# Full-size TensorE products that nothing reads, in the ramp of two self-attentions and in the tail of the first

## The chip, the cores and the metric

One core of a Trainium2 chip runs the whole decoder. The metric is the device time of one execution in microseconds (us), as the median of several runs. Everything below is about that one core and its engines: TensorE (PE, with its weight loads as PEld), VectorE (DVE), ScalarE (ACT), GpSimd (POOL) and SyncE (SP), which issues the DMAs. TensorE's clock has two levels, 2.4 GHz (1.00 in the profile's rows) and 1.2 GHz (0.50); which of them it was granted stands in each row of a table of stretches.

## The reference, cut to what matters

Two decoder layers over x of 4 x 1024 x 256. The stages are L0 self-attention, L0 cross-attention, L0 experts, L1 self-attention, L1 latent attention, L1 expert choice. The two self-attentions are what the change touches. Layer 0 is causal with 16 heads of 16; layer 1 is not causal and has 32 heads of 8, in couples whose results are subtracted:

```python
scores = jnp.einsum('bhqd,bhkd->bhqk', q, k) * scale        # L0: causal, masked above the diagonal
attn = jax.nn.softmax(scores, axis=-1)
out = jnp.einsum('bhqk,bhkd->bhqd', attn, v)
# L1: the same without a mask for (q1, k1) and (q2, k2); a = attn1 - lam * attn2
```

The softmax needs the largest score of every query before the exponentials, so the kernel computes the scores twice: once for the maxima, once, shifted by them, for the exponentials.

## The kernel before, in words

`attend` (line 338) does both self-attentions. The heads are taken in groups of four: 16 groups in L0 (4 batches x 4), 32 in L1. It is one program for each engine, all written out turn by turn by `run`: turn g does the maxima of group g ("new"), the exponentials and sums of group g-1 ("last") and the rest of those of group g-2 ("old"):

```python
for g in range(groups + 2):
    turn(At(g, None, 3), g < groups, 1 <= g <= groups, g >= 2)
```

A turn has NS steps, 12 in L0 and 16 in L1. In each step the PE program (`turn`, in `@block.tensor`) goes through s = 0 to 3, and for each s it issues one score of the group in hand (`score`, L727: keys as weights, 512 queries as columns, 64 rows in L0 and 32 in L1), one product for the maxima (`most`, L777: 62 or 30 rows, up to 512 columns), and after s = 1 and s = 3 half a step of the sums (`products`, `product`, L748: exponentials times V, four heads side by side on 32 columns of the array each). The two `most` of one pair fill one psM buffer, of which there are two; VectorE reduces it (L683; in L0 the pairs on the diagonal go through L677, which adds the mask), and the next pair but one waits for that on `m_read`. A turn has 2 NS pairs. The scores go to a ring of four psS banks, which ScalarE empties with the exponentials (L600) into `parts[0]` to `parts[2]`. In L0, POOL cuts the diagonal blocks of them (L563), and `product` waits for that.

The exponentials of a group begin LATE = 5 steps into the next turn, since its maxima first have to reach Q: after step 0 of that turn PE transposes them (`turn_maxima`, L786), ScalarE and POOL split them in two, SP copies them by eight DMAs into rows of Q (L508), and PE waits for those on `mx` at step 5. So there are three kinds of turn:

- **The ramp**, turn 0: maxima of group 0 alone. In turn 1, steps 0 to 4 are maxima alone as well (those of group 1); from step 5 on, scores, maxima and sums are mixed.
- **The turns between**: everything at once.
- **The tail**, turn `groups`: no maxima. Steps 0 to 4 are the last steps of the last group but one, steps 5 to 11 (in L0) the first steps of the last group. A short turn follows for its remaining steps.

Twice in a turn PE transposes a finished sum with four full 128 x 128 products (`turn_back`, L766). `parts[3]` is used in `project`, the stage before, for the projected queries and keys, and by nothing in `attend`. The psS banks are all free in turn 0.

Of the kernel before, what the change touches and what calls it, by code (L numbers as in the profile page):

```python
# [17 lines left out]
P = 128  # L18
# [4 lines left out]
HALF = 512  # L23
# [314 lines left out]
def attend(nc, a, keep, sems, tag, dh, groups, causal):  # L338
# [23 lines left out]
    pairs = []  # L362
# [5 lines left out]
    for s, (t, h) in order:  # L368
        keys = (t + 1) * P if causal else S
        n = min(HALF, keys - h * HALF)  # L370
        pairs.append((s, t, h, n, causal and h * HALF + n == keys))
    NS, NP2 = len(steps), len(pairs)
# [9 lines left out]
    with ExitStack() as ctx:  # L382
        m = Mem(nc, ctx)
        psM = [m.ps(f"{tag}_attn_psM{k}", 2 * HALF) for k in range(2)]
        psS = [m.ps(f"{tag}_attn_psS{k}", HALF) for k in range(4)]
# [36 lines left out]
        m_read = sems.sem(f"{tag}_attn_m_read")  # L422
# [6 lines left out]
        def run(turn):  # L429

            for g in range(groups + 2):
                turn(At(g, None, 3), g < groups, 1 <= g <= groups, g >= 2)

        def cuts(g, n):

            return g.times(4 * sum(diagonal), 4 * sum(diagonal[:n]))

        def in_turn(new, last):

            return range(NS if new or last else LATE + BACK + 4)  # L440

        taken, left, s_at = [], [], {}
        for g in range(1, groups + 2):
            new, last, old = g < groups, g <= groups, g >= 2
# [33 lines left out]
        def s_item(*key):  # L478

            return s_at[key], bank_of[key]  # L480

        def m_item(g, p):

            return g * NP2 + p, (g * NP2 + p) % 2

        with nc.Block() as block:
            @block.sync
            def _(sp):
                sp.dma_start(mask[:], a["causal"]).then_inc(maskin, 16)
                if shared == 2:  # L490
                    sp.dma_start(lam4[:], a[f"{tag}_lambda"].rearrange("(o k) d -> o k d", o=1).broadcast_to([P, 4, dh])).then_inc(lamin, 16)

                def turn(t, new, last, old):
                    if new and t.base >= 1:
                        if t.base == 3:
                            for k in range(4):
                                sp.wait_ge(parts_out[k], 256)
                        if t.base >= 3:
                            sp.wait_ge(s_done, s_at[t.base - 3, NS - 1, 3] + 1)
                        load_group(sp, keep, dh, t.base)  # L500
                    if last:

                        g = t + -1
                        sp.wait_ge(m_cut, g.times(2, 2))
                        for s in range(4):
                            c, r = head(s)
                            for j in range(2):
                                sp.dma_start(Q[g.slot][r + TOP + j:r + TOP + j + 1, c, :].bitcast(F32),  # L508
                                             mparts[g.slot][s * TB:(s + 1) * TB, j, :].bitcast(F32)).then_inc(mx[g.slot], 16)

                run(turn)
                for k in range(3):
                    n = len(range(k, groups, 3))
                    sp.wait_ge(mx[k], 128 * n)
# [202 lines left out]
            @block.tensor  # L717
            def _(pe):
                pe.sem_inc(o_done, RING)

                def score(g, n, s):
                    q, kt, c0 = steps[n]
                    c, r = head(s)
                    i, bank = s_item(g.base, n, s)

                    pe.wait_ge(e_done, order[g.base, n, s] + 1)
                    pe.matmul(psS[bank][:, c0:], K[g.slot][r:r + RH, c, kt * P:(kt + 1) * P],  # L727
                              Q[g.slot][r:r + RH, c, q * HALF + c0:(q + 1) * HALF], start=True, stop=True).then_inc(s_done, 1)

                def product(at, n, half):  # L730
                    g = At(at, None, 3)
                    q, kt, c0 = steps[n]
                    lo, hi = max(c0, half * HALF // HALVES), (half + 1) * HALF // HALVES
                    if lo >= hi:
                        return
                    if lo == c0:
                        if n == 0 or steps[n - 1][0] != q:

                            pe.wait_ge(e_done, order["O", at, q] + 1)
                        if n == 0:  # L740
                            pe.wait_ge(v_in, g.times(1, 1))

                        if diagonal[n]:
                            pe.wait_ge(e_cut, cuts(g, n + 1))
                        else:
                            pe.wait_ge(e_done, freed[at, n, 3])
                    for s in range(4):
                        last = pe.matmul(psS[bank_of["O", at, q]][32 * s:32 * s + 32, lo:hi], V[g.slot][:, kt, s // shared, :],  # L748
                                         E[(4 * n + s) % (4 * RING)][:, lo:hi], start=(kt == 0 and half == 0), stop=(n == ends[q]),
                                         skip_group_check=True)  # L750
                    if half == HALVES - 1:
                        last.then_inc(o_done, 1)

                def products(t, n, last, old, half):
                    j = n - LATE - BACK
                    if j >= 0 and last:
                        product(t.base - 1, j, half)
                    if j < 0 and old:
                        product(t.base - 2, NS + j, half)

                def turn_back(g, q):
                    i, bank = s_item("B", g, q)
                    pe.wait_ge(e_done, freed["O", g, q])
                    pe.wait_ge(e_done, order["B", g, q] + 1)
                    for j in range(4):
                        last = pe.transpose(psS[bank][:, j * P:(j + 1) * P], oT[q][:, j * P:(j + 1) * P], ident[:])  # L766
                    last.then_inc(s_done, 1)

                def most(t, p, j):
                    s, qt, h, n, _ = pairs[p]  # L770
                    i, bank = m_item(t.base, p)
                    if j == 1:

                        if i >= 2:
                            pe.wait_ge(m_read, i - 1)
                    c, r = head(s + j)
                    last = pe.matmul(psM[bank][:, j * HALF:j * HALF + n], Q[t.slot][r:r + TOP, c, qt * P:(qt + 1) * P],  # L777
                                     K[t.slot][r:r + TOP, c, h * HALF:h * HALF + n], start=True, stop=True)
                    if j == 0:
                        last.then_inc(m_done, 1)  # L780

                def turn_maxima(g):
                    i, bank = s_item("T", g)
                    pe.wait_ge(m_neg, g + 2)
                    pe.wait_ge(e_done, order["T", g] + 1)
                    pe.transpose(psS[bank][0:4 * TB, 0:P], negm[g % 3][:], ident[:]).then_inc(s_done, 1)  # L786

                def turn(t, new, last, old):
                    if new:
                        pe.wait_ge(ld[t.slot], t.over(LD, LD))  # L790
                    for n in in_turn(new, last):
                        k = n - LATE
                        g, step = (t + -1, k) if k >= 0 else (t + -2, NS + k)
                        live = last if k >= 0 else old
                        if last and k == 0:
                            pe.wait_ge(mx[g.slot], g.over(128, 128))
                        for s in range(4):
                            if live:
                                score(g, step, s)
                            if new:  # L800
                                most(t, 2 * n + s // 2, 1 - s % 2)
                            if (s + 1) * HALVES % 4 == 0:
                                products(t, n, last, old, (s + 1) * HALVES // 4 - 1)
                        if last and n == 0:
                            turn_maxima(t.base - 1)
                        if old and n == BACK1:
                            turn_back(t.base - 2, 1)
                        if last and n == BACK0:
                            turn_back(t.base - 1, 0)

                run(turn)
LAMBDA_INIT = 0.8 - 0.6 * math.exp(-0.3 * 12)
BLK = 4
# [2288 lines left out]
```

## Time and profile before

| | |
|---|---|
| median of 3 runs | 3541.02 us (3540.13 to 3545.2) |
| the profiled execution's own time | 3554.61 us |
| its span, from the first to the last instruction | 3552.9 us |
| mean granted TensorE clock | 0.92 |
| PE busy | 3169.2 us (89%) |
| DVE busy | 2786.6 us (78%) |
| ACT busy | 2104.8 us (59%) |
| L0 `attend`, first maximum to last sum | about 137 to 635 us of the span |
| L1 `attend` | about 1287 to 2557 us |

Busy time of PE counts any matmul in flight, at whichever clock. A matmul's duration is its latency: several overlap, so what one costs in a stream is the distance from one start to the next.

### The profile page before, as it was taken

To read this page: it belongs to the slowest core of one execution; us is meant where nothing else is said; L and a number is where in the kernel's file an instruction comes from. 1 tells how busy PE (TensorE), PEld (TensorE's weight loads), DVE (VectorE), ACT (ScalarE), POOL (GpSimd) and SP (SyncE) were. 2 spreads that over 40 slices of the span, in tenths; PEclk is the share of its full clock that TensorE was granted. 3 is DMA by queue.
4 is the path that set the end of the run, shared out by engine and by line. 5 is a ranking of instruction groups with operands and counts; after the bars stand their busy time and mean duration, and the time that the engine had idled before them with its cause. 6 is when DMAs were issued, how large, how long until landed. Compare 5 with 4: busy or idle time off the path is not lost. (4 is left out here: it accounts for less than half of the span.)

```text
span 3552.9 us, 63589 instructions
## 1 busy us (share of the span) xinstructions
PE 3169.2 (89%) x23976; PEld 1628.0 (46%) x23976; DVE 2786.6 (78%) x4742; ACT 2104.8 (59%) x4195; POOL 870.6 (25%) x1299
## 2 busy tenths in 40 slices
PE   7599999678499879999999999999856699999699
PEld 4244444444288533333333333343345455454556
DVE  7688885447577898999999999999366677776456
ACT  3178887245333217999999999999815333334130
POOL 4234433134333430000000000000112334445100
PEclk9689999879699977999999999999978899999789
DMA  5422220000000330100100001000002410100001
GB/s 170 127 54 62 66 58 20 27 0 1 25 1 1 118 113 20 29 20 21 29 20 24 25 20 28 22 20 20 4 9 81 169 50 28 48 26 1 17 0 48
DMA packets 69587, 144.08 MB, mean 41 GB/s; under 512 B 20864, under 2 KB 33984, under 8 KB 69152
## 3 DMA queue, kind: packets, MB, share of 16 engines
q1 hardware_dynamic: 64928, 135.82, 12.9%
q8 instruction: 189, 3.10, 0.4%
q10 hardware_dynamic: 4352, 4.20, 0.3%
q14 instruction: 118, 0.97, 0.1%
HBM read 83.19 MB, written 54.53 MB: 39 GB/s over the span
## 5 line engine op out<-in xcount | busy, mean ns | idle before, releaser
L600 ACT ACTIVATE L_parts<-L_attn_psS 128x512 f32<-128x512 f32 (+3 forms) x2816 | 1410.3, 574 | 151.1 <-PE L_attn_psS L727 109.4
L683 DVE TENSOR_REDUCE L_attn_tops<-L_attn_psM 128x2 f32<-128x1024 f32 x1152 | 1326.4, 1218 | 62.4 <-PE L_attn_psM L777 59.1
L777 PE MATMUL L_attn_psM<-L_K,L_Q 30*128 30x512 f32 (+4 forms) x2816 | 869.0, 492 | 67.6 <-PEq L199 31.7
L727 PE MATMUL L_attn_psS<-L_Q,L_K 32*128 32x512 f32 (+4 forms) x2816 | 880.8, 477 | 1.6 <-ACT L_parts L600 0.9
L748 PE MATMUL L_attn_psS<-L_parts,L_attn_V 128*32 128x256 f32 (+1 forms) x10752 | 860.0, 392 | 5.5 <-ACT L_parts L600 0.6
L727 PEld LDWEIGHTS L_attn_psS<-L_Q,L_K 32*128 32x128 f32 (+1 forms) x2816 | 410.0, 186 | 558.8 <-ACT L_parts L600 274.4
L777 PEld LDWEIGHTS L_attn_psM<-L_K,L_Q 30*128 30x128 f32 (+1 forms) x2816 | 391.1, 190 | 114.3 <-DVE L_attn_tops L683 58.2
L748 PEld LDWEIGHTS L_attn_psS<-L_parts,L_attn_V 128*32 128x32 f32 x10752 | 215.0, 108 | 357.0 <-issue 189.0
L677 DVE CUSTOM_DVE_ANT_0 L_attn_psM<-L_attn_psM,L_attn_wide 128x384 f32<-128x384 f32 (+3 forms) x512 | 236.7, 523 | 20.2 <-PE L_attn_psM L777 19.7
L2357 ACT ACTIVATE x_E<-x_psS 128x512 f32<-128x512 f32 x256 | 139.0, 596 | 173.6 <-PE x_psS L2480 154.2
L2403 DVE TENSOR_REDUCE x_tops<-x_psM 128x2 f32<-128x1024 f32 x128 | 153.1, 1206 | 87.2 <-PE x_psM L2509 87.1
L2319 POOL TENSOR_TENSOR x_acc<-x_acc,x_E 128x512 f32<-128x512 f32 x128 | 172.1, 1344 | 171.5 <-ACT x_E L2357 169.2
L1557 PE MATMUL m_psE<-m_wp,m_xp 128*128 128x512 f32 x768 | 182.1, 394 | 2.8 <-DVE m_z L1691 2.8
L563 POOL TENSOR_SCALAR_AFFINE_SELECT L_parts<-L_parts 128x128 f32<-128x128 f32 x512 | 146.3, 294 | 129.9 <-ACT L_parts L600 123.2
L554 POOL TENSOR_TENSOR L_attn_mparts<-L_attn_mT,L_attn_mparts 32x128 fp32r<-32x128 f32 x48 | 21.6, 450 | 623.9 <-ACT L_attn_mT L609 623.9
L542 POOL TENSOR_TENSOR L_attn_recs<-L_attn_rec,L_attn_sign 128x16 f32<-128x16 f32 x64 | 14.3, 223 | 634.1 <-DVE L_attn_rec L694 634.1
L1557 PEld LDWEIGHTS m_psE<-m_wp,m_xp 128*128 128x128 f32 x768 | 142.6, 189 | 34.6 <-DVE m_z L1691 5.8
L2476 PE MATMUL x_psS<-x_Q,x_K 64*128 64x512 f32 x864 | 148.0, 431 | 11.6 <-ACT x_E L2357 11.4
L2529 PE MATMUL x_psO<-x_E,L1x_VL 128*64 128x512 f32 x512 | 139.9, 625 | 0.0
L2509 PE MATMUL x_psM<-x_K,x_Q 64*128 64x512 f32 x768 | 117.9, 405 | 24.5 <-DMA x_K<-L1x_kTc 21.4
L324 PE MATMUL L_proj_psQ<-L_AO,L_proj_wqk 128*128 128x512 f32 x256 | 124.1, 611 | 16.9 <-DMA L_AO<-in_L_sin 12.6
L2476 PEld LDWEIGHTS x_psS<-x_Q,x_K 64*128 64x128 f32 x864 | 73.7, 186 | 139.8 <-ACT x_E L2357 91.7
(370 smaller groups left out, 4083.6 us busy)
## 6 DMA issues: line engine op xcount, KB each, us to landing
parts_q<-L_parts SPq DMA_DIRECT2D x64, 256.0 KB
parts_k<-L_parts SPq DMA_DIRECT2D x64, 256.0 KB
L_Q<-parts_q SPq DMA_DIRECT2D x192, 64.0 KB
L_K<-parts_k SPq DMA_DIRECT2D x192, 64.0 KB
L_Q<-parts_q SPq DMA_DIRECT2D x64, 128.0 KB
L_K<-parts_k SPq DMA_DIRECT2D x64, 128.0 KB
queries<-x1p_qo SPq DMA_DIRECT2D x16, 512.0 KB, 3.8
keys<-x1p_ko SPq DMA_DIRECT2D x16, 512.0 KB, 4.2
```

What stands on the lines that cost most here:

```text
L563: pool.affine_select(block, block, [[1, P]], ALU.is_ge, 0.0, base=0, channel_multiplier=-1).then_inc(e_cut, 1)
L600: act.activation(E[(4 * n + s) % (4 * RING)][:, c0:], psS[bank][:, c0:], ACT.Exp, scale=scale).then_inc(e_done, 1)
L677: last = dve.tensor_tensor_reduce(part, part, wide[:, HALF - n:], 1.0, LOWEST, ALU.add, ALU.max, tops[:, row, h:h + 1])
L683: dve.tensor_reduce(dst, src, AX, ALU.max).then_inc(m_read, 1)
L727: pe.matmul(psS[bank][:, c0:], K[g.slot][r:r + RH, c, kt * P:(kt + 1) * P], Q[g.slot][r:r + RH, c, q * HALF + c0:(q + 1) * HALF], start=Tr ...
L748: last = pe.matmul(psS[bank_of["O", at, q]][32 * s:32 * s + 32, lo:hi], V[g.slot][:, kt, s // shared, :], E[(4 * n + s) % (4 * RING)][:, l ...
L777: last = pe.matmul(psM[bank][:, j * HALF:j * HALF + n], Q[t.slot][r:r + TOP, c, qt * P:(qt + 1) * P], K[t.slot][r:r + TOP, c, h * HALF:h * ...
L1557: last = pe.matmul(psE[e][:], xp[u.slot][:, i, c, k * P:(k + 1) * P], wp[:, j, c, e * HALF:(e + 1) * HALF], start=(n + c == 0), stop=(n == ...
L2319: pool.tensor_tensor(to[:], to[:], e[:], ALU.add).then_inc(sums[1], 1)
L2403: dve.tensor_reduce(dst[:, :, t, h], src, AX, ALU.max).then_inc(m_read, 1)
L2476: pe.matmul(banks[h][:], K[k][rows, x, kt * P:(kt + 1) * P], Q[k][rows, y, cols], start=(j == 0), stop=False, skip_group_check=True)
L2529: last = pe.matmul(psO[LD * h:LD * h + LD, :], v, tile(s, h)[:], start=(kt == 0), stop=(kt == TB), skip_group_check=True)
```

## The change

`busy(bank)` is one matmul with a full 128 x 128 block of `parts[3]` as weights and 512 columns of it, all of the type of Q and K, into a bank that nothing reads. It is issued in two places of PE's `turn`:

- in turn 0 of both layers, after each pair of maxima, once for every full 256 columns of the pair (0, 1 or 2 times), into psS[3]: in L0 32 in all (of the 12 pairs of each half, six have 512 columns, two 384, two 256, two 128), in L1 64, two for each of the 32 pairs;
- in turn 16 of L0, after s = 1 and after s = 3 of each of the 12 steps, once, into half of psM[0]: 24. The first of them has a wait of its own ahead of it, until VectorE has read the last maxima.

```diff
+                def busy(bank):
+
+                    idle = keep["parts"][3]
+                    pe.matmul(bank, idle[:, 0, 0:P], idle[:, 0, HALF:], start=True, stop=True, skip_group_check=True)
+
                 def turn_maxima(g):
...
                             if new:
                                 most(t, 2 * n + s // 2, 1 - s % 2)
+                            if new and not last and s % 2 == 1:
+                                for _ in range(pairs[2 * n + s // 2][3] // 256):
+                                    busy(psS[3][:])
+                            if causal and last and not new and s % 2 == 1:
+                                if n == 0 and s == 1:
+                                    pe.wait_ge(m_read, groups * NP2)
+                                busy(psM[0][:, 0:HALF])
                             if (s + 1) * HALVES % 4 == 0:
                                 products(t, n, last, old, (s + 1) * HALVES // 4 - 1)
```

Nothing is removed or moved.

## Rows read from the trace of the kernel before

**Rows 1.** The page: PE busy, and its clock in 40 slices.
```profile
PE   7599999678499879999999999999856699999699
PEclk9689999879699977999999999999978899999789
```

**Rows 2.** Stretches of L0 and L1 `attend`: length, busy us (instructions) of engines, clock.
```profile
core 0: us, PE busy (x) PEld busy (x) DVE busy (x) ACT busy (x) POOL busy (x), PEclk, DMA share, GB/s
137.00:167.00 30.00, 14.93 (x48) 6.86 (x48) 24.06 (x70) 0.00 (x0) 4.18 (x8) 0.50 0.29 80
167.00:178.00 11.00, 6.41 (x22) 3.12 (x22) 10.14 (x30) 0.43 (x2) 0.45 (x1) 0.50 0.10 26
...
1286.00:1324.00 38.00, 24.86 (x66) 9.19 (x66) 36.20 (x38) 1.49 (x2) 2.41 (x8) 0.50 0.15 43
1324.00:1334.00 10.00, 7.18 (x19) 2.39 (x18) 9.93 (x10) 0.42 (x2) 0.79 (x2) 0.50 0.05 13
1341.00:1369.00 28.00, 28.00 (x200) 7.97 (x196) 19.78 (x17) 18.09 (x34) 0.00 (x0) 0.50 0.01 1
...
1374.00:1400.00 26.00, 25.92 (x277) 10.23 (x269) 25.41 (x24) 24.68 (x50) 3.40 (x8) 1.00 0.13 33
```

**Rows 3.** Stretches by scores alone (L727): length, PE and PEld busy, clock.
```profile
178.00:201.35 23.35, 12.25 (x28) 6.50 (x28) 0.50 0.24 58
241.00:257.35 16.35, 9.68 (x28) 4.73 (x28) 1.00 0.35 98
574.70:591.15 16.45, 9.68 (x28) 4.77 (x28) 1.00 0.01 1
601.50:622.40 20.90, 10.54 (x28) 4.38 (x28) 0.59 0.00 1
563.40:574.65 11.25, 6.23 (x20) 3.07 (x20) 1.00 0.02 5
591.20:601.40 10.20, 5.14 (x20) 2.55 (x20) 1.00 0.02 6
1334.70:1373.30 38.60, 18.75 (x44) 6.78 (x43) 0.50 0.07 17
2479.50:2505.80 26.30, 13.39 (x44) 6.13 (x44) 1.00 0.01 1
```

**Rows 4.** PE in order of time, L1 ramp: start, length, what [idle before].
```profile
1291.39 0.80 PE L777 MATMUL L_attn_psM<-L_K,L_Q 30*128 30x512 f32 x2 [0.34 <-DVE L_attn_tops L683]
1292.52 0.80 PE L777 MATMUL L_attn_psM<-L_K,L_Q 30*128 30x512 f32 x2 [0.34 <-DVE L_attn_tops L683]
```

**Rows 5.** Who DVE waited for in 143 to 166 us (L0 ramp): us, times, longest.
```profile
DVE L_attn_tops L683 <- PE L_attn_psM L777: 0.8, 2, 0.4
DVE L_attn_psM L677 <- PE L_attn_psM L777: 0.8, 2, 0.4
```

**Rows 6.** PE in order of time, L1 turn 1 to 2, around the clock's rise.
```profile
1371.37 1.08 PE L748 MATMUL L_attn_psS<-L_parts,L_attn_V 128*32 128x256 f32 x8
1372.38 1.04 PE L766 MATMUL L_attn_psS<-ident,L_attn_oT 128*128 128x128 f32 x4
1373.35 0.49 PE L727 MATMUL L_attn_psS<-L_Q,L_K 32*128 32x512 f32 x1
```

**Rows 7.** PE in order of time, L0 experts: full-size products.
```profile
972.59 4.70 PE L1557 MATMUL m_psE<-m_wp,m_xp 128*128 128x512 f32 x17
...
1039.82 2.44 PE L1557 MATMUL m_psE<-m_wp,m_xp 128*128 128x512 f32 x10
```

**Rows 8.** Two stretches of L0 cross-attention, columns as in rows 2.
```profile
834.00:844.00 10.00, 7.24 (x34) 4.07 (x27) 7.23 (x10) 7.86 (x17) 5.61 (x4) 1.00 0.01 2
844.00:850.00 6.00, 6.00 (x36) 2.77 (x34) 5.42 (x13) 2.77 (x6) 3.50 (x2) 0.72 0.00 1
```

**Rows 9.** Stretches of L0's tail, columns as in rows 2.
```profile
592.00:601.00 9.00, 9.00 (x95) 3.88 (x91) 0.22 (x1) 7.97 (x22) 4.73 (x15) 1.00 0.02 6
601.00:605.00 4.00, 3.25 (x24) 1.19 (x16) 0.00 (x0) 3.08 (x8) 2.06 (x8) 1.00 0.01 3
605.00:619.00 14.00, 13.74 (x83) 5.22 (x84) 0.25 (x1) 8.93 (x22) 3.92 (x13) 0.51 0.00 1
619.00:622.00 3.00, 3.00 (x22) 0.94 (x21) 0.00 (x0) 2.17 (x4) 0.00 (x0) 0.50 0.00 0
622.00:632.00 10.00, 10.00 (x104) 4.43 (x106) 0.25 (x1) 8.48 (x21) 4.49 (x15) 0.99 0.01 2
```

**Rows 10.** PE in order of time, L0 tail, end of step 4 and start of step 5.
```profile
600.79 0.64 PE L748 MATMUL L_attn_psS<-L_parts,L_attn_V 128*32 128x256 f32 x8
601.60 0.73 PE L727 MATMUL L_attn_psS<-L_Q,L_K 64*128 64x512 f32 x3 [0.16 <-DMA L_Q<-L_attn_mparts]
```

## The prediction

> **What bounds the kernel now.** The page first: PE is busy in most slices (of 88.8 us each), and its clock is below 9 tenths in some, among them the 2nd and 3rd and the 15th and 16th [rows 1]. Those hold the starts of the two `attend` stages. The table of stretches then shows what goes on there.
>
> The L1 ramp (1286 to 1324 us) ran at 0.50 throughout, but VectorE was busy 36.20 of 38.00 us [rows 2]: it sets the pace, and the slow clock costs nothing. In order of time, the two maxima of a pair start together, take 0.80 us, and PE then sits idle for 0.34 us until VectorE has freed a buffer; a pair comes every 1.13 us (1291.39 to 1292.52) [rows 4]. Steps 0 to 4 of turn 1 look the same: VectorE 9.93 of 10.00 us, PE 7.18. Only from step 5 on does the clock matter: from 1341 to 1369 us PE was busy all 28.00 us, VectorE 19.78, ACT 18.09, still at 0.50; after 1374, at 1.00, VectorE and ACT are both near their full share [rows 2].
>
> What that costs can be read by the same piece of work at both clocks. Scores of steps 0 to 10 of group 0 of L1 (44 of them) took 38.60 us, those of group 30 took 26.30: 12.3 us. Steps 0 to 6 of group 0 of L0 took 23.35 us, of group 2 16.35: 7.0 us. In L0's tail steps 0 to 6 of the last group took 20.90 us, of the group before (with maxima beside them) 16.45: 4.45 us [rows 3]. So 23.8 us are to be had, all three in places where scores run, none in the ramps themselves.
>
> What PE did before the clock moved: in L1 it stayed at 0.50 through 28 us of gapless scores, maxima and sums, and rose right after four full-size transposes had joined them (1372.38; at 1373.35 a score takes 0.49 us) [rows 2, 6]. In the experts it rose a moment into a run of full-size products (17 in 4.70 us from 972.59) [rows 7]. So full-size work does raise it. It fell where PE was still at work but lightly: in cross-attention after a stretch with 7.24 of 10.00 us busy [rows 8], in L0's tail after 601 to 605 us with 3.25 of 4.00 [rows 9]. It isn't idleness alone that lets it fall.
>
> **The change, part by part.** One added product costs, at 1.00, the distance between such products in a stream: ten in 2.44 us, less the last one's latency of about 0.39, over nine, is 0.23 us [rows 7]; at 0.50 twice that, 0.46.
>
> *L1 ramp, 64 products.* At 0.50 a pair then takes PE 512 columns at 1.2 GHz, 0.43 us (the two maxima run side by side), and 2 x 0.46: 1.35 us against VectorE's 1.13, so 0.22 us more for each pair while the clock is low. Full-size work is then two thirds of PE's time, more than in the mix that raised the clock at 1372, so I expect it to rise within some five pairs: +1.1 us. From there PE needs 0.21 + 0.46 = 0.67 us of 1.13: nothing. Ends: 0, and 32 x 0.22 = +7.0 if it never rises. Taken: +1.
>
> *L0 ramp, 32 products.* At 0.50 all of PE's work is at most 24 x 0.43 + 32 x 0.46 = 25.0 us beside 24.06 us of VectorE's in a stretch of 30 [rows 2]; the pairs with 128 columns get none, so PE catches up. VectorE waited for PE 1.6 us in 143 to 166 [rows 5], part of which goes if the clock is high. Ends: -1.6 and +3. Taken: 0.
>
> *Turn 1 of both layers.* The added products stop with turn 0. Then come five steps of maxima alone, 11 us in L0 (167 to 178) and 10 to 11 in L1 (1324 to 1334.7), in which PE does what it did before the change: x22 and x19 instructions of 62 or 30 rows [rows 2]. At 1.00 they are half as long, so PE is at work less than the 7.24 of 10.00 us after which the clock fell in cross-attention [rows 8]. I take it that the clock is back at 0.50 before the first score at 178.0 and 1334.8, and both losses (7.0 and 12.3) stay. Taken: 0. The other end is -19.3.
>
> *L0 tail, 24 products.* The clock fell at about 605, after PE had waited for the maxima's DMAs and with small diagonal steps to do [rows 9, 10]. Two full-size products in each step are 0.46 us more work in about 2 us, and the lightest stretch is no longer light: I expect it to stay at 1.00, worth up to 4.45 us. Against it stands their own time. In steps 0 to 4, ten products, at most 10 x 0.23 = 2.3 us; ACT is busy 7.97 of 9.00 us there [rows 9], so part of it hides. The `turn_maxima` of step 0 is queued behind two of them, so the DMAs that PE waits for at 601.60 (0.16 us idle, PE had hardly arrived earlier [rows 10]) land up to 0.46 us later. Taken: +0.9. In steps 5 to 11, fourteen products, at most 3.2 us; but the 16.45 us of the group before had 28 maxima and VectorE's pace in it [rows 3], which are gone. Taken: 0 against that 16.45. The added wait on `m_read` is met: all of PE's later work is queued behind it, but VectorE has done with the maxima as turn 16 begins (one instruction of 0.22 us in 592 to 601 [rows 9]), and `turn_maxima` of the same step waits for later work of VectorE anyway. The stage after starts with the end of this chain, so a gain here is a gain of the whole. Sum of the tail: -4.45 + 0.9 = -3.5. Ends: -4.45, and -4.45 + 2.3 + 3.2 = +1.1.
>
> **Sum.** +1 + 0 + 0 - 3.5 = -2.5 us. The profiled execution took 3554.61 us (span 3552.9), 13.6 above the median; against it this gives 3552.1. The difference carries over to the median of 3541.02: 3538.5 us. A measurement of this kernel can tell about 0.2%, 7.1 us, from no change, so this is "same".
>
> **The rivals.** *A: the clock is carried through the maxima of turn 1.* Then the scores of both layers begin at 1.00, -19.3 us more: 3519. This holds if the clock falls only where PE is idle, since in 1324 to 1334 it never is for long. Against it: both falls in rows 8 and 9 came with PE at work for 72 and 81% of the time [rows 8, 9]. The Trainium skill ("TensorE: Matmul & The Clock Gate", section "Why this matters for your kernels") states just such a rule: throughput drops are avoided by leaving no long idle gaps between bursts of matmuls. By that rule this case comes out; the falls in rows 8 and 9 speak against it, and so does the 28 us of unbroken work at 0.50 against its companion, that staying busy raises the clock [rows 2]. Chance 0.12.
>
> *B: the products don't move the clock.* They are of another kind than transposes, and may count for less. Then PE paces the L1 ramp at 1.35 us a pair (+7.0), the L0 ramp loses up to 3 (say +1.5), and the tail falls to 0.50 as before, where PE is the bound (13.74 of 14.00 us busy [rows 9]) and fourteen products at 0.46 are open: +6.4, with +0.9 before. Sum +15.8: 3557. It decides from the point where less than half of that holds, since +7.1 is already slower. For it: PE has no slack at 0.50. Against: rows 6 and 7. Chance 0.1.
>
> *C: the tail gives back what it gains.* The clock stays, but in the small diagonal steps PE, not ACT, is the bound (9.00 of 9.00 us busy in 592 to 601, [rows 9]), so most of the 24 products are open: +1.1 there, +1 in L1: 3543; half of it, 3541. Chance 0.2.
>
> **How the numbers follow.** My forecast has 0.58. Its own range is 3534 to 3543: the tail's -4.45 with -1.6 of the L0 ramp below, the spread of runs (5 us here) around it. C lies inside it. The range of 3530 to 3547 holds both, 0.78, and the nearer part of B and A's edge. Faster by over 0.2% (below 3533.9): A, and 0.08 of the forecast's lower edge, 0.2. Slower (above 3548.1): B, 0.1. The rest, 0.7.
>
> **What would show it.** In the profile after: the clock rises in each ramp (1.00 for most of 1295 to 1324), VectorE's pair stays at 1.13 us; the clock is 0.50 again by 1334 and the 44 scores of L1's group 0 still take about 38 us, the 28 of L0's about 23; in L0's tail there is no fall at 605 and the last group's 28 scores take about 16.5 us. I am wrong if group 0's scores take 26 us (A), if the ramp of L1 is longer by 5 us or more (B), or if the tail's 28 scores take over 19 us at a high clock (C).

## The result

The changed kernel took 3582.16 us (median of 4 executions, 3579.7 to 3585.45) against 3543.11 us for the kernel before (4 executions, 3540.13 to 3550.42): a ratio of 1.0101, 95% interval 1.0084 to 1.0118. By that ratio it is 36 us slower (the two medians are 39 us apart), where 2.5 us faster was forecast. The profiled execution took 3579.7 us, its span 3578.0.

The stretches of the changed kernel, columns as in rows 2; the first two answer to the L1 ramp and to steps 0 to 4 of turn 1 there, the last two to rows 9:

```profile
1294.00:1353.00 59.00, 59.00 (x128) 24.83 (x126) 39.20 (x37) 1.49 (x2) 1.63 (x7) 0.50 0.08 20
1353.50:1363.50 10.00, 6.81 (x21) 2.53 (x21) 9.50 (x11) 0.42 (x2) 0.78 (x2) 0.50 0.08 19
...
596.00:608.00 12.00, 12.00 (x100) 4.72 (x92) 0.00 (x0) 8.14 (x22) 5.08 (x16) 1.00 0.01 3
609.00:627.00 18.00, 18.00 (x128) 7.93 (x127) 0.25 (x1) 13.67 (x31) 5.20 (x17) 1.00 0.00 1
```

Two things are to be seen. The L1 ramp is now 60 us long instead of 37, PE is busy in all of it and VectorE in two thirds: PE has become the pace. And the clock is still 0.50, for all 59 us. Who VectorE waited for in that stretch (us in total, times, longest):

```profile
DVE L_attn_tops L683 <- PE L_attn_psM L777: 20.3, 32, 0.9
```

PE in order of time in the ramp, the changed kernel (L785 is the added product):

```profile
1312.14 0.79 PE L777 MATMUL L_attn_psM<-L_K,L_Q 30*128 30x512 f32 x2
...
1312.86 1.22 PE L785 MATMUL L_attn_psS<-L_parts 128*128 128x512 f32 x2
...
1314.01 0.28 PEld L777 LDWEIGHTS L_attn_psM<-L_K,L_Q 30*128 30x128 f32 x2 [0.65 <-issue]
1314.01 0.79 PE L777 MATMUL L_attn_psM<-L_K,L_Q 30*128 30x512 f32 x2
```

A pair comes every 1.87 us (1312.14 to 1314.01; 1.13 in rows 4). The two maxima have 0.43 us of columns, yet the first full-size product starts 0.72 us after them (1312.14 to 1312.86). The next maxima start 1.15 us after that (1312.86 to 1314.01), for 2 x 0.43 us of columns. So 3 x 0.43 + 2 x 0.29 = 1.87: the excess of 0.29 us comes twice a pair, where 30 rows give way to 128 and where 128 give way to 30. It is about as long as the weight load there (0.28).

The scores of group 0 and the tail, columns as in rows 3:

```profile
595.00:608.50 13.50, 4.29 (x20) 1.84 (x20) 1.00 0.02 4
608.50:627.30 18.80, 7.54 (x28) 3.32 (x28) 1.00 0.00 1
187.40:205.80 18.40, 9.32 (x28) 4.95 (x28) 0.75 0.35 73
1364.00:1397.40 33.40, 17.27 (x44) 6.69 (x43) 0.64 0.06 18
```

In the tail the clock held, as forecast, but steps 0 to 4 took 13.5 us instead of 10.2 and the last group's 28 scores 18.8 instead of the 16.45 hoped for.

### The profile page after: what moved, and what is told of

The parts are those of the page before. It is cut to its first block and busy times, and to the rows that moved or that the text cites. A ratio compares the mean times of both kernels' runs of the same rounds, so it can differ in the third digit from the quotient of the medians.

```text
span 3578.0 us, 63829 instructions
## 1 busy us (share of the span) xinstructions
PE 3218.1 (90%) x24096; PEld 1652.9 (46%) x24096; DVE 2790.6 (78%) x4742; ACT 2102.8 (59%) x4195; POOL 870.9 (24%) x1299
## 5 line engine op out<-in xcount | busy, mean ns | idle before, releaser
L777 PE MATMUL L_attn_psM<-L_K,L_Q 30*128 30x512 f32 (+4 forms) x2816 | 863.3, 490 | 44.0 <-PEq L199 31.3
L727 PE MATMUL L_attn_psS<-L_Q,L_K 32*128 32x512 f32 (+4 forms) x2816 | 871.1, 472 | 0.7 <-DMA L_Q<-L_attn_mparts 0.5
L748 PE MATMUL L_attn_psS<-L_parts,L_attn_V 128*32 128x256 f32 (+1 forms) x10752 | 850.9, 388 | 5.6 <-ACT L_parts L600 0.6
L727 PEld LDWEIGHTS L_attn_psS<-L_Q,L_K 32*128 32x128 f32 (+1 forms) x2816 | 405.7, 184 | 548.5 <-ACT L_parts L600 262.5
L2488 PE MATMUL x_psS<-x_Q,x_K 64*128 64x512 f32 x864 | 148.9, 434 | 11.6 <-ACT x_E L2369 11.4
```

The lines of the kernel that those rows point to most:

```text
L2488: pe.matmul(banks[h][:], K[k][rows, x, kt * P:(kt + 1) * P], Q[k][rows, y, cols], start=(j == 0), stop=False, skip_group_check=True)
```

## The experiments

All stage times below are from one trace each, in us: *R0*, *R1* from the first maximum to the first score of group 0 in L0 and L1 (turn 0 and steps 0 to 4 of turn 1); *S0*, *S1* the 28 and 44 scores of rows 3; *T* L0's tail, from step 0 of turn 16 to the last group's step 7. Medians and ratios are over all executions. Each ratio is against executions of the kernel before that ran beside that run, not against the table's first row; their medians were 3545.82 us (25 executions; before_again to burst_before_scores), 3548.98 (35; the two after that, burst_end_of_ramp and tail_late), 3550.04 (23; ramp_same_rows and burst_in_mix) and 3548.11 (17; combined).

| kernel | median (n) | ratio, 95% interval | R0 | S0 | R1 | S1 | T |
|---|---|---|---|---|---|---|---|
| before, first trace | 3543.11 (4) | | 40.7 | 23.4 | 47.9 | 38.6 | 31.4 |
| the change | 3582.16 (4) | 1.0101, 1.0084 to 1.0118 | 48.6 | 18.4 | 70.7 | 33.4 | 32.4 |
| before_again | 3545.23 (10) | 0.9999, 0.9977 to 1.0020 | 42.1 | 20.0 | 47.8 | 30.6 | 31.3 |
| ramp_only | 3580.73 (4) | 1.0090, 1.0055 to 1.0125 | 48.4 | 20.3 | 70.7 | 28.4 | 31.2 |
| tail_only | 3550.09 (10) | 1.0015, 0.9997 to 1.0034 | 42.3 | 20.3 | 47.9 | 29.4 | 32.4 |
| burst_before_scores | 3553.15 (10) | 1.0016, 0.9993 to 1.0040 | 46.3 | 15.7 | 54.0 | 33.9 | 27.1 |
| ramp_grouped | 3552.32 (10) | 1.0013, 0.9997 to 1.0029 | 44.7 | 20.8 | 51.7 | 31.7 | 27.5 |
| ramp_low_rows | 3557.08 (10) | 1.0017, 0.9996 to 1.0037 | 48.9 | 21.0 | 47.8 | 38.6 | 30.1 |
| burst_end_of_ramp | 3554.72 (10) | 1.0016, 0.9996 to 1.0037 | 45.3 | 21.1 | 51.8 | 35.4 | 25.8 |
| tail_late | 3550.12 (12) | 1.0007, 0.9991 to 1.0023 | 41.9 | 21.0 | 47.9 | 38.5 | 28.1 |
| ramp_same_rows | 3549.04 (10) | 0.9993, 0.9976 to 1.0009 | 41.9 | 21.0 | 47.8 | 31.9 | 27.4 |
| burst_in_mix | 3543.86 (12) | 0.9987, 0.9968 to 1.0006 | 42.5 | 22.3 | 47.9 | 31.8 | 31.3 |
| combined | 3546.61 (12) | 0.9991, 0.9973 to 1.0010 | 41.7 | 20.6 | 47.8 | 32.0 | 28.1 |

**before_again.** No edit.

> The kernel before, unchanged, to see what varies in it: its profiled execution took 3554.6 us, its others 3540 to 3550. Theory 1 (the clock in the mixed part of turn 1 rises at a varying moment): an execution near 3541 us shows group 0's scores of L1 (44, 38.6 us in the first profile) or of L0 (28, 23.4 us) shorter, together by about 10 us, because TensorE's clock rises earlier. Theory 2 (the spread lies elsewhere, in the experts or the last stages): both stretches take 38 to 39 and 23 to 24 us again.

Its profiled execution took 3544.41 us, 10.2 less than the first. L1's 44 scores (1326.2 to 1356.8), columns as in rows 3:

```profile
1326.20:1356.80 30.60, 16.49 (x44) 6.76 (x44) 0.74 0.08 21
```

The clock rose at 1342 us, step 5 of group 0, with no transposes near. The 8.0 us less in S1 and the 3.4 us less in S0 are 11.4 us, all of the difference: theory 1. In the four traces in which nothing is added up to the end of L1's first scores (before, before_again, tail_only, tail_late) S1 runs from 29.4 to 38.6 us. So the loss of 12.3 us in rows 3 is the upper end of what executions show, and the late rise in it, right after four transposes [rows 6], is no proof that these had caused it.

**ramp_only** and **tail_only.** One half of the change each: the other `if` of the diff is left out.

> The change without the tail's 24 products. Theory 1 (the price is the switch between maxima of 30 or 62 rows and full-height products, whose weights load in the open, 0.29 us each at the low clock, on an engine that was already near VectorE's pace): 1.87 us a pair in the L1 ramp, +24 us there and +8 in L0's, nearly the whole of the change's loss, 3575 to 3583 us. Theory 2 (most of the loss is from the tail, by its wait and its products): at most +20, under 3563 us.

> The change without the ramps' 96 products. Theory 1 (in the tail the clock is kept, and what that gives is eaten by 24 products at about 0.43 us each, twice the 0.23 us that a stream of them showed): within 3 us of before, clock 1.00 from 592 to 632 us, 28 scores of the last group in about 19 us. Theory 2 (the tail carries a large part of the loss): +15 us or more.

The ramp's 96 products carry 0.9 of the 1.0%: R1 is 22.8 us longer, R0 6 to 8. That is theory 1 of ramp_only in its sizes; it doesn't yet show that the wait is a weight load. For tail_only the clock and the 18.8 us for 28 scores are as in theory 1, and theory 2's +15 us lies outside the interval (-1 to +12 us), which however can't confirm "within 3 us". With the tail's products T is 32.4 in both traces that have all 24; without any, in nine traces, 25.8 to 31.4, 29.2 in the mean. The products do keep the clock up to the last of these scores, and against that mean they cost 3 us more than that gives.

**ramp_grouped.** The same products, in fours after two pairs.

```diff
-                            if new and not last and s % 2 == 1:
-                                for _ in range(pairs[2 * n + s // 2][3] // 256):
+                            if new and not last and s == 3:
+                                for _ in range(pairs[2 * n][3] // 256 + pairs[2 * n + 1][3] // 256):
```

> The ramp's 96 products as in the change, no tail products, but those of two pairs of maxima together after the second pair: the same products, half the switches between maxima and full-height products. Theory 1 (each switch leaves one weight load of 0.29 us in the open): two pairs take 2 x 0.43 + 4 x 0.43 + 2 x 0.29 = 3.16 us instead of 2 x 1.87 = 3.74; the 32 pairs of L1's ramp take about 51 us instead of 60. Theory 2 (a full-height product costs 0.72 us wherever it stands): 60 us as before.

PE in order of time, first at the low clock, then at the high one:

```profile
1293.85 0.80 PE L777 MATMUL L_attn_psM<-L_K,L_Q 30*128 30x512 f32 x4
1294.58 2.07 PE L785 MATMUL L_attn_psS<-L_parts 128*128 128x512 f32 x4
1296.58 1.31 PE L777 MATMUL L_attn_psM<-L_K,L_Q 30*128 30x512 f32 x4
...
1299.83 0.80 PE L777 MATMUL L_attn_psM<-L_K,L_Q 30*128 30x512 f32 x4
...
1305.34 0.50 PE L777 MATMUL L_attn_psM<-L_K,L_Q 30*128 30x512 f32 x2 [0.21 <-DVE L_attn_tops L683]
1305.77 1.20 PE L785 MATMUL L_attn_psS<-L_parts 128*128 128x512 f32 x4
```

Two periods of two pairs take 5.98 us (1293.85 to 1299.83), 2.99 each: near theory 1's 3.16 (four maxima of L1 can fit side by side, which saves some) and far from 3.74. Within a group the products come every (1.20 - 0.50) / 3 = 0.23 us at the high clock, the stream's price of the prediction; the first of them starts 0.43 us after the maxima, 0.22 more than their 0.21 us of columns. And now the clock did rise: at 1288.4 for 3.4 us, then at 1302.1 up to the ramp's end. In L0 it rose for 3.4 us alone (155.2), and R0 is 44.7. R1 fell from 70.7 to 51.7, the kernel's loss from 0.9% to 0.13% (an interval that takes in none). L1's ramp alone, from the first maximum of group 0 to that of group 1, took 40.9 us, where theory 1 had 51 and the change 60: it had reckoned with the low clock throughout. So half the switches took away more than half of the loss, partly by the clock. That the switches had held the clock down before is argued, not shown.

**ramp_low_rows** and **ramp_same_rows.** The ramp's products on fewer rows.

```diff
-                    pe.matmul(bank, idle[:, 0, 0:P], idle[:, 0, HALF:], start=True, stop=True, skip_group_check=True)
+                    pe.matmul(bank, idle[96:P, 0, 0:P], idle[96:P, 0, HALF:], start=True, stop=True, skip_group_check=True)
```

and `idle[P - RH:P, ...]` (64 rows in L0, 32 in L1) in the second.

> The ramp's 96 products of the same 512 columns and 128 output rows, but on rows 96 to 128 only, no tail products. Theory 1 (the switch between heights is what costs): no load in the open, so a pair of L1's ramp stays at 1.13 to 1.3 us and the kernel within 6 us of before. Theory 2 (the number of products and columns costs, whatever their height): 1.87 us a pair and +30 us or more, as with full height.

> The ramp's 96 products on as many rows as the maxima beside them take up (64 in L0, 32 in L1), no tail products. With 32 rows in both layers L1's ramp kept its pace but L0's showed 1.87 us a pair (maxima of 62 rows). Theory 1 (a weight load is in the open where two neighbours differ in height, whichever is taller): now L0's pairs are near VectorE's pace too, from the first maximum to the first score in 41 to 44 us instead of 48.9, and L1 as before, 48 us. Theory 2 (in L0 any 512 columns more on PE are too much, for its pairs are short): 47 to 49 us again in L0.

PE in order of time in L0's ramp, ramp_low_rows and then ramp_same_rows:

```profile
153.16 0.79 PE L777 MATMUL L_attn_psM<-L_K,L_Q 62*128 62x512 f32 x2
153.88 1.21 PE L785 MATMUL L_attn_psS<-L_parts 32*128 32x512 f32 x2
155.02 0.79 PE L777 MATMUL L_attn_psM<-L_K,L_Q 62*128 62x512 f32 x2
```

```profile
151.11 0.79 PE L777 MATMUL L_attn_psM<-L_K,L_Q 62*128 62x512 f32 x2 [0.15 <-DVE L_attn_tops L677]
151.70 0.62 PE L785 MATMUL L_attn_psS<-L_parts 64*128 64x512 f32 x1
151.88 0.79 PE L777 MATMUL L_attn_psM<-L_K,L_Q 62*128 62x512 f32 x1
```

With 32 rows beside 62 the pair takes 1.86 us, as with 128 beside 62 or 30; with 64 beside 62, or 32 beside 30, the products slip in between and the ramps are as long as before the change (R0 41.9, R1 47.8; ratio 0.9993). In the ramps it isn't the number of products, nor their size, but the change of height between neighbours. That is what I had not priced. Free as they were, these products did nothing for the clock; L1's ramp in ramp_same_rows, columns as in rows 2:

```profile
1281.00:1318.00 37.00, 36.43 (x128) 23.04 (x128) 35.64 (x37) 1.49 (x2) 2.42 (x8) 0.50 0.14 41
```

In the tail the price falls without a change of height too. The changed kernel there, scores, added product, sums, at the high clock:

```profile
596.40 0.49 PE L727 MATMUL L_attn_psS<-L_Q,L_K 64*128 64x512 f32 x2
596.82 0.50 PE L785 MATMUL L_attn_psM<-L_parts 128*128 128x512 f32 x1
597.26 0.64 PE L748 MATMUL L_attn_psS<-L_parts,L_attn_V 128*32 128x256 f32 x8
```

From the added product to the sums it is 0.44 us for 0.21 of columns, and both have 128 rows. They differ in width (128 and 32 columns) and in type (float32r and float32 in the kernel); no run tells which of the two costs.

The Trainium skill ("TensorEngine Tiling (Array Packing)", section "Tiling Modes") states that changing the tiling mode, as against only the tile, makes the TensorEngine drain. The traces agree in where the price falls, at a change of the shape in rows or columns, with 0.29 us a change at the low clock and 0.22 at the high one. That what passes in it is a drain, they don't show.

**burst_end_of_ramp**, **burst_before_scores** and **burst_in_mix.** No products in ramp and tail; 14, 14 or 10 back to back, after step 15 of L1's turn 0 (step 11 in L0), after step 4 of turn 1, and ahead of the first score of step 3 of group 0.

```diff
+                        if new and not last and n == NS - 1:           # burst_end_of_ramp
+                        if last and not old and n == LATE - 1:         # burst_before_scores
+                            for _ in range(14):
+                                busy(psS[3][:])
...
                     pe.wait_ge(e_done, order[g.base, n, s] + 1)
+                    if g.base == 0 and n == 3 and s == 0:              # burst_in_mix
+                        for _ in range(10):
+                            busy(psS[bank][:])
```

> No product in ramp or tail but 14 full-size ones back to back after the last pair of turn 0, in both layers. Theory 1 (the clock rises with them and falls again during the maxima of turn 1, steps 0 to 4): 1.00 for some us, 0.50 again before the first score of group 0, whose 44 scores in L1 then take 30 to 39 us as before; the kernel is slower by the 5 to 10 us that the products take from VectorE. Theory 2 (rival A of the prediction, the clock is carried through these maxima): the 44 scores take 26 to 28 us and the 28 of L0 16 to 17.

> No product in ramp or tail; in their place 14 full-size products back to back at the end of step 4 of turn 1, right before the first scores, in both layers. Theory 1 (full-size products raise the clock when they come without gaps, and the mix of scores, maxima and sums then keeps it): the clock rises during or just after the 14 (some 6 us at the low clock), and the 44 scores of L1's group 0 take about 27 us, the 28 of L0's about 17. Net about -5 to -15 us against before, since the 14 cost 4 to 6 us in each layer. Theory 2 (this kind of product doesn't raise the clock at all): it stays at 0.50, the scores take as long as before, and the kernel is 6 to 12 us slower.

> No product in ramp or tail but 10 full-size ones back to back ahead of the first score of step 3 of group 0, in the midst of the mixed work of turn 1 (the burst ahead of the first scores raised the clock in L1 for 3.4 us only, then the light first steps let it fall). Theory 1 (the full mix keeps a clock that is raised within it): 1.00 from step 3 or 4 on in both layers without a fall; the 44 scores of L1 take 28 to 31 us with 4 to 5 us of them for the burst, the 28 of L0 18 to 20; 0 to 5 us faster than before, most of the gain paid for by the burst. Theory 2 (the mix doesn't keep it): a fall within 10 us and 3 to 10 us slower.

Stretches of L1 in burst_end_of_ramp, columns as in rows 2 (the first score of group 0 is at 1330.7):

```profile
1319.00:1325.00 6.00, 3.53 (x17) 1.60 (x16) 4.08 (x4) 0.42 (x2) 0.78 (x2) 1.00 0.01 2
1326.00:1331.00 5.00, 3.63 (x11) 1.36 (x9) 5.00 (x5) 0.00 (x0) 0.00 (x0) 0.50 0.26 69
```

The burst raised the clock, and it was gone again with the maxima of turn 1, before the first score; in L0 the same (1.00 from 165 to 172, first score at 176). This speaks against the prediction's rival A, as argued. The burst ahead of the scores raised it for only 3.4 us in L1, whose first mixed steps are light (PE at work 2.00 of 3.00 us, 1336 to 1339), but for the rest of the scores in L0 (S0 15.7, the shortest of all). So its theory 1 held for L0's stage and not for L1's (S1 33.9, where 27 was expected); the bursts lengthened the ramps by 4 to 6 us each, and the 5 to 15 us of gain did not come (ratio 1.0016). PE in order of time in burst_in_mix:

```profile
1332.31 3.51 PE L788 MATMUL L_attn_psS<-L_parts 128*128 128x512 f32 x10
1335.75 0.50 PE L730 MATMUL L_attn_psS<-L_Q,L_K 32*128 32x512 f32 x1
```

Here the clock rose within the burst, at 1334.4, and the full mix kept it to the end of the stage (1.00 from 1334.5 to 2542). S1 is 31.8 with the burst in it, which lies within the 29.4 to 38.6 of traces without one. In L0 the clock rose too (184.1), but S0 is 22.3, more than the 18 to 20 of theory 1: nothing gained. The ratio's interval, 0.9968 to 1.0006, takes in none.

**tail_late.** Eight products, steps 5 to 8 alone (`LATE <= n < LATE + 4` in the second `if`, the wait at n == LATE).

> No product in the ramps; in the tail of L0 only 8, in steps 5 to 8 of turn 16 (after s = 1 and s = 3), where the clock fell. Theory 1 (the tail's products are worth it only where the clock would fall; the ten in steps 0 to 4 cost 3 us for nothing): steps 0 to 4 take 10.4 us as before, no fall at the waiting point, the last group's 28 scores in 17 to 18 us against 21; 2 to 4 us faster than before, which its spread may hide. Theory 2 (eight are too few): the clock falls all the same, 28 scores in 22 us or more, 1 to 3 us slower.

Steps 0 to 4 took 10.3 us, the 28 scores 17.8, and the clock did not fall up to the last of these scores: T 28.1, the sizes of theory 1. But tails without any product took 25.8 to 31.4, as the fall in them comes and goes, and 28.1 lies in the middle of that. So that the eight products shorten the stage is not shown; the kernel's time (1.0007) doesn't show it either.

**combined.** tail_late, and burst_in_mix in L1 alone.

> The two edits that paid in their stage, without the others: 8 products in steps 5 to 8 of L0's tail, and the burst of 10 ahead of step 3's first score of group 0, in L1 alone (in L0 it gained nothing). Theory 1 (the gains add up): L0's tail from step 0 to the last group's step 7 in about 28 us instead of 31.4, L1's 44 scores in about 32 us with the clock up from the burst on; together 4 to 8 us faster than before, 0.1 to 0.2%, at the edge of what its spread lets through. Theory 2 (the clock of before rises early by itself in most executions, so the burst pays only in some): 0 to 3 us faster.

T 28.1 and S1 32.0 are as intended, but both lie within what traces without the edits show. The ratio of 0.9991, 3 us, has an interval from 10 us faster to 4 us slower: no gain can be told from none. The kernel before beats the change, and nothing that I tried clearly beats the kernel before.

## Why the prediction was wrong

- *One product at 0.23 or 0.46 us.* This is the step that failed. The price was read from a stream of products of one shape [rows 7] and used for products that stand alone between others of another height. Such a product costs a change of shape more: 0.43 us for one in the tail at the high clock (0.21 + 0.22), and (1.87 - 0.43) / 2 = 0.72 us for each of the two in a ramp's pair at the low one (0.43 + 0.29). The price of a stream was right (0.23 in ramp_grouped, within a group). The kernel before showed the rest, had I looked for it; two scores with two maxima, then sums, then scores at the low clock:

```profile
1342.81 0.79 PE L777 MATMUL L_attn_psM<-L_K,L_Q 30*128 30x512 f32 x1
1343.53 0.20 PEld L748 LDWEIGHTS L_attn_psS<-L_parts,L_attn_V 128*32 128x32 f32 x8 [0.44 <-issue]
1343.53 1.08 PE L748 MATMUL L_attn_psS<-L_parts,L_attn_V 128*32 128x256 f32 x8
1344.54 0.79 PE L727 MATMUL L_attn_psS<-L_Q,L_K 32*128 32x512 f32 x1
```

  0.72 us from the last 32-row pair to the sums, for 0.43 us of columns. The excess is again 0.29 us, though all eight weight loads of the sums take 0.20. So the "weight load in the open" of my expectations has the right size beside the maxima (0.28) and not here: the price of a change is shown, what fills it stays open.
- *L1 ramp, +1, with +7 as the upper end.* It cost 22.8 us: 32 x (1.87 - 1.13) = 23.7. The expected rise of the clock within five pairs did not come. "Full-size work is two thirds of PE's time" counted columns; with the two waits of 0.29 us in each pair it was 0.86 of 1.87 us. The same products in groups did raise it. Its other support, that transposes had raised the clock at 1372, has against it that in before_again it rose at 1342 with none near.
- *L0 ramp, 0.* It cost 6 to 8 us for the same reason: the heights of its neighbours alone take that away (R0 41.9 in ramp_same_rows, 48.9 in ramp_low_rows).
- *Turn 1, 0.* The mechanism was right: the clock is at 0.50 when the scores begin, and burst_end_of_ramp shows that a raised one doesn't last. But when it rises afterwards varies from execution to execution, so S0 and S1 of one trace say little.
- *L0 tail, -3.5.* The clock held, as forecast. The term for steps 0 to 4 was +0.9 and measured +3.3; steps 5 to 11 took 18.8 instead of 16.45. Against the first trace the tail is +1.0, rival C's figure, though by a dearer product than C had; against the mean of nine traces +3.2.
- *Rival B* had the right side and the right pace-setter, but the wrong reason (in groups and bursts these products do raise the clock) and less than half the price, 3557 us.
- *The bound of 0.2%.* The four executions first shown lie close. Over 35 of the kernel before the times run from 3527 to 3562 us, about 1%, and even 10 or 12 executions against 17 to 35 leave an interval of about 0.2% to either side.

In stages the change is +22.8 +7 in the ramps and +1 to +3 in the tail, 31 to 33 us; the median's ratio gives 36, 30 to 42.

## What to carry to other kernels

Before adding or moving a small matmul, look at the shapes of its neighbours: each change of height cost more than the columns here, 0.29 us at the low clock and 0.22 at the high one, and so did the step from 128 x 128 to the sums' 128 x 32. Put such products together, or give them the height of what stands beside them; in these ramps, where VectorE sets the pace, they then cost nothing. They bought nothing either: no filler here paid. A burst raised the clock, and where the full mix followed at once it stayed up, but it gave back no more than the burst itself took.

## What was not expected

- The mix of turn 1 raises the clock by itself, at a moment that differs between executions: S1 from 29.4 to 38.6 us, S0 from 20.0 to 23.4. This, and the tail's fall that one trace out of nine did not show at all (T 25.8 to 31.4), makes up to some 18 us (9.2 + 3.4 + 5.6) of the kernel's spread of 35. Where the rest lies was not looked for.
- The change of height costs in both directions and also from 62 to 32 rows, both less than full: 1.86 us a pair. And it comes with no change of height at all, between the tail's added products and the sums.
- PE busy 59.00 of 59.00 us at 0.50, with full-size products in every pair of it: neither their presence nor an unbroken busy row was enough to raise the clock here.
- What in the first mixed steps of L1 let the clock fall after burst_before_scores was only argued, not tried.
